# A fused attention, RWKV and feed-forward layer on one core: a new opening, new engine orders, and four second feed-forwards whose residual is added in SBUF

## The chip, the cores and the metric

The kernel runs on 1 core of one Trainium2 chip. The metric is the device time of one execution in microseconds (us). Before the change it is 283.79 us, the median of 3 runs (283.71 to 286.62).

## What is computed

Eight batches of 512 tokens with 128 channels pass through four blocks, each added to its own input. All data is f32.

```python
x = L0_attn_a_hidden_states                       # [8, 512, 128]
x = x + attn(_layernorm(x), W_q)                  # (y Wq^T) y^T y, without softmax
x = x + ffn(_layernorm(x), ...)                   # first feed-forward
x = x + rwkv(_layernorm(x), ...)                  # time mix with a scan over tokens, then channel mix
x = x + ffn(_layernorm(x), ...)                   # second feed-forward, same weights
...
def ffn(tgt):                                     # only expert 0 of 8 has weight 1
    h = relu(tgt @ w1 + b1)
    z = tgt + (h @ w2 + b2)
    return (z - mean(z)) * rsqrt(var(z) + 1e-5) * gamma + beta
```

## The kernel before, in words

One program runs on five in-order engines: TensorE (PE), VectorE (DVE), ScalarE (ACT), GpSimd (POOL) and the DMA queue of SyncE (SP). They meet by semaphores only. Nothing is scheduled by a compiler: each engine's part of the file ends in a long list of calls, written out by hand, such as `attn_gram(1, 3)`, which is batch 1 into PSUM bank 3. That list is the order in which the engine works. Extra arguments on PE's calls, such as `x1.ready(0)`, are waits for the former user of the bank.

The residual stream of batch b stays in SBUF in `R[b]`, 128 partitions by 4 groups by 128 channels. One batch goes through these stages:

- Attention: `attn_stats` and `mean_var` on DVE (L394, L422), `shift`, `power`, `bias` on POOL (L269, L293, L297; the reciprocal root and the bias of the norm), `attn_normed` on ACT, which writes XN (L678). Then PE: `attn_gram` (L918), `attn_transpose` (L906), `attn_proj` (L926) and `attn_apply` (L933), with copies out of PSUM on ACT between them, and `attn_out` on DVE (L428), which makes x1.
- A feed-forward (f1, later f2): the same norm gives y (`ffn_normed`), PE transposes it (`ffn_transpose`, L906), ACT evacuates it as yT and adds the centred bias B2C (L730). Four `hidden_up` (L945) and `relu` (L738) make h. The sum z = y + b2 + h W2 is collected in one bank: `ffn_start` (L952) transposes yT back into the bank, four small transposes, and four `ffn_down` (L961) of four products each add to it. DVE takes `z_stats` (L394), `mean_var`, and after POOL's `z_shift` (L288) and `power` (L293) `ffn_scaled` (L440), which writes zg. POOL issues a DMA that adds beta to R (`ffn_residual`, L321) and one that adds zg to R (`ffn_sum`, L329); for batch 0 of f1 and batch 7 of f2 DVE does the latter (`ffn_add`, L447). SP stores batch b when this is done.
- Time mix and channel mix: transposes and products on PE (L975 to L1020), scans and elementwise work on DVE, exponentials and squares on ACT, small norms and the adding DMAs (L337, L344) on POOL.

The opening: SP loads x0 of batches 0, 1 and 2 among the first weights. PE runs 42 transposes of the identity (`warm_up`, L1026), `centre_bias` (L1032) and then batch 0. `centre_down_bias` (DVE, L582) reads what `centre_bias` wrote. `ffn_y` has two copies per feed-forward, h has one.

Of the kernel before, what the change touches and what calls it, by code (L numbers as in the profile page):

```python
# [24 lines left out]
def hybrid_layer(nc, hidden, w_q, w1, w2, b1, wk, wv, wr, wo, f_wk, f_wr, f_wv, vectors, gamma, beta, out):  # L25
# [5 lines left out]
    with ExitStack() as ctx:  # L31
# [83 lines left out]


        class Norm:


            def __init__(self, n, dst=None, dst_name="", steps=("ve", "rs", "nb")):  # L120
# [6 lines left out]
                self.scale = Steps(n + "_scale_steps", 1, *steps)  # L127
                self.dst = dst
                if dst is not None:
                    self.nm = copies(n + "_nm", [P, J], 2)  # L130
                    self.nb = copies(n + "_nb", [P, J], 2)
                    self.ready = Steps(dst_name + "_ready", 1, "but last", "all")

        class Ffn:


            def __init__(self, n, stage, x):
                self.stage = stage
# [71 lines left out]
        def _(sp):  # L210
# [37 lines left out]
        def _(pool):  # L248
# [73 lines left out]

            def ffn_sum(b, f, tile):
# [7 lines left out]
            def cmix_sum(b):
# [19 lines left out]
            power(2, f1.norm); ffn_residual(1, f1); bias(2, f1.norm); shift(3, f1.norm); power(3, f1.norm)
            bias(3, f1.norm); ffn_residual(2, f1); ffn_residual(3, f1); z_shift(0, f1); power(0, f1.znorm)
            shift_twice(0); power(0, nt); back_shift(0); bias(0, nt); back_power(0); z_shift(1, f1); back_scale(0)
            power(1, f1.znorm); shift(4, f1.norm); power(4, f1.norm); ffn_sum(1, f1, f1.zg); bias(4, f1.norm)
            ffn_residual(4, f1); shift_twice(1); power(1, nt); back_shift(1); bias(1, nt); z_shift(2, f1)
            back_power(1); power(2, f1.znorm); back_scale(1); ffn_sum(2, f1, f1.zg); shift_twice(2); power(2, nt)
            tmix_residual(0); back_shift(2); back_power(2); shift(0, ncm); power(0, ncm); z_shift(3, f1); bias(0, ncm)
            back_scale(2); power(3, f1.znorm); shift(5, f1.norm); power(5, f1.norm); ffn_sum(3, f1, f1.zg)
            bias(5, f1.norm); bias(2, nt); ffn_residual(5, f1); z_shift(4, f1); power(4, f1.znorm); shift_twice(3)
            ffn_sum(4, f1, f1.zg); power(3, nt); bias(3, nt); back_shift(3); tmix_residual(1); back_power(3)  # L360
            shift(1, ncm); power(1, ncm); back_scale(3); bias(1, ncm); shift(6, f1.norm); power(6, f1.norm)
            shift_twice(4); bias(6, f1.norm); power(4, nt); shift(7, f1.norm); bias(4, nt); power(7, f1.norm)
            ffn_residual(6, f1); z_shift(5, f1); bias(7, f1.norm); power(5, f1.znorm); cmix_sum(0)
            ffn_sum(5, f1, f1.zg); shift(0, f2.norm); power(0, f2.norm); ffn_residual(7, f1); bias(0, f2.norm)
            shift_twice(5); z_shift(6, f1); ffn_residual(0, f2); power(6, f1.znorm); power(5, nt); bias(5, nt)
# [5 lines left out]
            shift_twice(7); power(7, nt); shift(2, f2.norm); bias(7, nt); power(2, f2.norm); tmix_residual(4)
            bias(2, f2.norm); back_shift(6); shift(4, ncm); power(4, ncm); ffn_residual(2, f2); bias(4, ncm)
            back_power(6); back_scale(6); z_shift(1, f2); power(1, f2.znorm); cmix_sum(3); ffn_sum(1, f2, f2.zg)
            shift(3, f2.norm); power(3, f2.norm); bias(3, f2.norm); back_shift(7); back_power(7); z_shift(2, f2)
# [805 lines left out]
```

## Time and profile before

| what | us |
|---|---|
| median of 3 runs | 283.79 |
| the profiled execution, its own time | 286.06 |
| its span, first to last instruction | 284.3 |
| PE busy | 263.8 (93%) |
| ACT busy | 229.8 (81%) |
| DVE busy | 227.1 (80%) |
| POOL busy | 148.5 (52%) |

The span is what the trace covers. The profiled execution's own time is 1.8 us longer than its span and 2.3 us above the median. A change is worked out in the span's microseconds and taken off the median. Ends of matmuls are modelled in the profile, so the distance from one start to the next is used as a matmul's cost.

### The profile page before, as it was taken

The numbers are of one execution on the slowest core, as the hardware profiler recorded it, in microseconds if no ns is written. First come the engines' busy times: TensorE is split into PE (matmuls) and PEld (weight loads), VectorE is DVE, ScalarE is ACT, GpSimd is POOL, SyncE is SP. The second block draws the span as 40 slices with busy tenths as digits, with TensorE's granted clock in tenths as the row PEclk, the third lists the DMA queues.
The fourth block names the chain that finished last, engine by engine and source line by source line (L and its number), as shares of the span: only waits on it lengthen the run. The fifth ranks groups of instructions, "written<-read, shape, count | busy, mean of one in ns | idle before, by whom it ended". The sixth has DMA issues, their size and how long they took to land. (4 is left out here: it accounts for less than half of the span.)

```text
span 284.3 us, 5322 instructions
## 1 busy us (share of the span) xinstructions
PE 263.8 (93%) x1556; PEld 196.6 (69%) x1556; DVE 227.1 (80%) x739; ACT 229.8 (81%) x443; POOL 148.5 (52%) x294
## 2 busy tenths in 40 slices
PE   7598999997996999999999999999999989999990
PEld 7598688566684577477665676866757848777770
DVE  1648616889999999999999999999998499754224
ACT  2486994966598989997999998998999998788630
POOL 3474934654192599285882661953922524851331
PEclk9959999999999999999999999999999999999997
DMA  6910340220124122244404303225351405643132
GB/s 185 310 53 0 56 81 15 40 37 13 24 39 75 26 51 37 39 76 74 74 1 77 74 16 60 37 47 105 55 108 26 75 0 110 115 98 78 25 61 74
DMA packets 17740, 18.10 MB, mean 64 GB/s; under 512 B 1456, under 2 KB 11568, under 8 KB 17712
## 3 DMA queue, kind: packets, MB, share of 16 engines
q0 software_dynamic: 6480, 11.80, 24.3%
q1 hardware_dynamic: 11232, 5.97, 7.4%
q8 instruction: 12, 0.20, 0.3%
q14 instruction: 16, 0.13, 0.1%
HBM read 3.87 MB, written 2.10 MB: 21 GB/s over the span
## 5 line engine op out<-in xcount | busy, mean ns | idle before, releaser
L961 PEld LDWEIGHTS bank<-W,f_h 128*128 128x128 f32 x512 | 61.3, 192 | 9.9 <-issue 9.2
L961 PE MATMUL bank<-W,f_h 128*128 128x128 f32 x512 | 63.1, 275 | 0.3 <-ACT f_h L738 0.3
L945 PE MATMUL bank<-f_yT,W 128*128 128x512 f32 x128 | 62.6, 599 | 0.1
L738 ACT ACTIVATE f_h<-bank,B1C 128x512 f32<-128x512 f32 x64 | 42.5, 684 | 9.5 <-PE bank L945 9.3
L1003 PE MATMUL bank<-XK,FWk 128*128 128x512 f32 x64 | 32.2, 607 | 2.8 <-DVE XK L559 1.4
L945 PEld LDWEIGHTS bank<-f_yT,W 128*128 128x128 f32 x128 | 21.7, 190 | 18.3 <-issue 12.3
L1009 PEld LDWEIGHTS bank<-FWv,KK 128*128 128x128 f32 x256 | 30.5, 192 | 4.8 <-issue 2.2
L1009 PE MATMUL bank<-FWv,KK 128*128 128x128 f32 x256 | 31.2, 276 | 0.2 <-ACT KK L799 0.2
L394 DVE BATCH_NORM_STATS2 f_zn_stats<-bank 128x6 f32<-128x128 f32 x64 | 14.1, 282 | 18.3 <-PE bank L961 18.2
L678 ACT ACTIVATE f_y<-R,f_yn_nb,f_yn_rs 128x128 f32<-128x128 f32 x64 | 26.3, 485 | 2.6 <-POOL f_yn_nb L297 2.3
L440 DVE SCALAR_TENSOR_TENSOR f_zg<-bank,f_zn_rs,GAMMA 128x128 f32<-128x128 f32 x64 | 17.9, 341 | 7.6 <-issue 5.6
L329 POOL DMA_DIRECT2D R<-f_zg x14 | 12.9, 920 | 19.1 <-DVE f_zg L440 19.1
L321 POOL DMA_DIRECT2D R<-BETA x16 | 14.4, 899 | 14.0 <-ACT f_y L678 13.6
L795 ACT ACTIVATE KK<-bank 128x512 f32<-128x512 f32 x32 | 18.8, 595 | 3.5 <-PE bank L1003 3.4
L799 ACT ACTIVATE KK<-KK 128x512 f32<-128x512 f32 x32 | 19.8, 634 | 0.3
L678 ACT ACTIVATE XN<-R,attn_nb,attn_rs 128x128 f32<-128x128 f32 x32 | 13.1, 485 | 8.6 <-POOL attn_nb L297 8.6
L293 POOL TENSOR_TENSOR f_zn_rs<-f_zn_ve,K_RSQRT 128x4 f32<-128x4 f32 x16 | 17.8, 1114 | 0.8
L1003 PEld LDWEIGHTS bank<-XK,FWk 128*128 128x128 f32 x64 | 10.4, 190 | 10.7 <-issue 5.1
L293 POOL TENSOR_TENSOR f_yn_rs<-f_yn_ve,K_RSQRT 128x4 f32<-128x4 f32 x16 | 16.7, 1046 | 0.0
L269 POOL TENSOR_TENSOR f_yn_ve<-f_yn_mv,K_EPS 128x4 f32<-128x4 f32 x16 | 4.1, 256 | 21.6 <-DVE f_yn_mv L422 21.6
L288 POOL TENSOR_TENSOR f_zn_ve<-f_zn_mv,K_EPS 128x4 f32<-128x4 f32 x16 | 5.7, 356 | 18.1 <-DVE f_zn_mv L422 17.9
L678 ACT ACTIVATE NC<-N,cmix_nb,cmix_rs 128x128 f32<-128x128 f32 x32 | 13.2, 488 | 2.1 <-POOL cmix_nb L297 2.1
(133 smaller groups left out, 619.2 us busy)
## 6 DMA issues: line engine op xcount, KB each, us to landing
R<-BETA POOLq DMA_DIRECT2D x16, 256.0 KB, 3.5
R<-f_zg POOLq DMA_DIRECT2D x14, 256.0 KB, 3.4
R<-in_hidden SPq DMA_DIRECT2D x8, 256.0 KB, 4.7
R<-N POOLq DMA_DIRECT2D x8, 256.0 KB, 3.3
out_x<-R SPq DMA_DIRECT2D x8, 256.0 KB, 2.3
R<-G POOLq DMA_DIRECT2D x7, 256.0 KB, 3.4
W<-in_w SPq DMA_DIRECT2D x2, 256.0 KB, 4.5
BETA<-in_beta SPq DMA_DIRECT2D x1, 256.0 KB, 5.2
```

The lines of the kernel that those rows point to most:

```text
L293: pool.tensor_tensor(n.rs[b % 2][:], n.ve[b % 2][:], K_RSQRT[:], ALU.pow).then_inc(n.scale.sem(b), 1)
L321: pool.dma_start(R[b][:], BETA[:], accum_op=ALU.add).then_inc(*f.xb.step(b))
L394: last = v.bn_stats(n.stats[b % 2][:, j, :], src[:, j, :])
L440: last = v.scalar_tensor_tensor(zg[:, j, :], z[:, j, :], f.znorm.rs[b % 2][:, j:j + 1], GAMMA[:], ALU.mult, ALU.mult)
L678: done = a.activation(dst[:, j, :], src[:, j, :], ACT.Identity, scale=n.rs[b % 2][:, j:j + 1], bias=n.nb[b % 2][:, j:j + 1])
L738: a.activation(at(f.h, b)[:, n, :], banks[bank][:], ACT.Relu, bias=B1C[:, n:n + 1]).then_inc(f.h_ready[n], 1)
L795: a.activation(at(KK, b)[:, n, :], banks[bank][:], ACT.Relu).then_inc(square[n].sem(b), 1)
L799: a.activation(at(KK, b)[:, n, :], at(KK, b)[:, n, :], ACT.Square).then_inc(square[n].sem(b), 1)
L945: t_.matmul(banks[bank][:], W1[:, n * P:(n + 1) * P], at(f.yT, b)[:], start=True, stop=True).then_inc(f.h_psum[n], 1)
L961: last = t_.matmul(banks[bank][:, j * C:(j + 1) * C], at(f.h, b)[:, n, j * P:(j + 1) * P], W2[:, n, :], start=False, stop=(n == H - 1), sk ...
L1003: t_.matmul(banks[bank][:], FWk[:, n * P:(n + 1) * P], at(XK2, b)[:], start=True, stop=True).then_inc(kk_psum[n], 1)
L1009: last = t_.matmul(banks[bank][:, j * C:(j + 1) * C], at(KK, b)[:, n, j * P:(j + 1) * P], FWv[:, n, :], start=(n == 0 and j == 0), stop=(n ...
```

## The change

- Opening. PE's 42 warm-up transposes become 24, then `centre_bias`, then 20. On DVE the statistics of batch 1 move ahead of `centre_down_bias`. XN of batch 0 is written by DVE (a new `attn_normed`) instead of ACT. SP loads x0 of batch 3 ahead of B1 and W1. Four batches, not seven, have their attention products ahead of the first `hidden_up`; batches 4 to 7 follow between feed-forwards.
- All engine orders, and the banks that PE uses, are written anew. y has four copies and h two. Some semaphores are split in two so that neighbouring batches can pass.
- In f2, for batches 1, 3, 5 and 6, `ffn_start` is gone. `ffn_down` opens the bank itself. A new POOL DMA `down_residual` adds b2 (as rows, B2R) onto y in SBUF once y is transposed. DVE adds the bank to y (`z_sum`), takes the statistics from SBUF and scales in place (`z_sum_scaled`).
- For f1 batch 0 and f2 batch 7, `ffn_scaled` and `ffn_add` become `ffn_gain`, one product with gamma that doesn't wait for the norm, and `ffn_out`, which scales and adds into R.
- B2R is made once: `bias_diagonal` on DVE, `down_bias_part` on PE, `down_bias_rows` on ACT.

```diff
-COPIES = {"N": 3, "f1_y": 2, "f2_y": 2, "f1_yT": 2, "f2_yT": 2, "XN": 3, "XNT": 2, "GRAM": 2, "PROJ": 2, "f1_zg": 3, "f2_zg": 3, "others": 1}
+COPIES = {"N": 3, "f1_y": 4, "f2_y": 4, "f1_yT": 2, "f2_yT": 2, "f1_h": 2, "f2_h": 2, "XN": 3, "XNT": 2, "GRAM": 2,
+          "PROJ": 2, "f1_zg": 3, "f2_zg": 3, "others": 1}
+SPLIT = {"f1": (0,), "f2": (7,)}
+IN_SBUF = {"f2": (1, 3, 5, 6)}
...
+            load_x0(3)
             sp.dma_start(B1[:], b1).then_inc(w1_loaded, DMA)
             sp.dma_start(W1[:], w1).then_inc(w1_loaded, DMA)
-            load_x0(3)
...
+            def down_residual(b, f):
+
+                if b == f.in_sbuf[0]:
+                    pool.wait_ge(b2_rows, 1)
+                pool.wait_ge(f.yT_psum, b + 1)
+                for earlier in f.yb.before(b):
+                    pool.wait_ge(*earlier)
+                pool.dma_start(at(f.y, b)[:], B2R[:], accum_op=ALU.add).then_inc(*f.yb.step(b))
...
+            def z_sum(b, f, bank):
+
+                dve.wait_ge(f.z_psum, b + 1)
+                dve.wait_ge(*f.yb.ready(b))
+                v.tensor_tensor(at(f.y, b)[:], bank_rows(bank), at(f.y, b)[:], ALU.add).then_inc(f.z_ready, 1)
...
+            def ffn_gain(b, f, bank):
...
+                v.tensor_tensor(at(f.zg, b)[:], bank_rows(bank), GAMMA[:].unsqueeze(1).broadcast_to([P, J, C]), ALU.mult).then_inc(f.zg_ready, 1)
+
+            def ffn_out(b, f):
+
+                dve.wait_ge(*f.znorm.scale.done(b, "rs"))
+                dve.wait_ge(f.zg_ready, b + 1)
+                dve.wait_ge(*f.xb.ready(b))
+                for j in range(J):
+                    last = v.scalar_tensor_tensor(R[b][:, j, :], at(f.zg, b)[:, j, :], f.znorm.rs[b % 2][:, j:j + 1], R[b][:, j, :],
+                                                  ALU.mult, ALU.add)
...
+            def attn_normed(b):
+
+                dve.wait_ge(na.mv_ready, b + 1)
+                dve.wait_ge(*na.scale.done(b, "rs"))
+                dst = at(XN, b)
+                for j in range(J):
+                    done = v.tensor_scalar(dst[:, j, :], R[b][:, j, :], na.mv[b % 2][:, j, 0:1], na.rs[b % 2][:, j:j + 1], ALU.subtract, ALU.mult)
...
+                    if b - len(f.y) in f.in_sbuf:
+                        act.wait_ge(*f.out.ready(b - len(f.y)))
...
-                    last = t_.matmul(banks[bank][:, j * C:(j + 1) * C], at(f.h, b)[:, n, j * P:(j + 1) * P], W2[:, n, :], start=False,
+                    last = t_.matmul(banks[bank][:, j * C:(j + 1) * C], at(f.h, b)[:, n, j * P:(j + 1) * P], W2[:, n, :], start=(n == 0 and j == 0 and b in f.in_sbuf),
```

PE from its start, before. IDENT x42 is the warm-up, XN alone is `attn_gram`, IDENT,XN is `attn_transpose`, GRAM,Wq is `attn_proj`, B2C,W is `bias_part`, PROJ,XNT is `attn_apply`.

```order
L1026 MATMUL bank<-IDENT 128x128 x42
L1032 MATMUL bank<-VEC,MEAN 128x1
L906 MATMUL bank<-IDENT,XN 128x128 x4
L918 MATMUL bank<-XN 128x128 x4
L906 MATMUL bank<-IDENT,XN 128x128 x4
L918 MATMUL bank<-XN 128x128 x4
L926 MATMUL bank<-GRAM,Wq 128x128
L1039 MATMUL bank<-B2C,W 128x1 x4
L906 MATMUL bank<-IDENT,XN 128x128 x4
L918 MATMUL bank<-XN 128x128 x4
L933 MATMUL bank<-PROJ,XNT 128x128 x4
```

The same place in the change, by the changed file's line numbers.

```order
L1113 MATMUL bank<-IDENT 128x128 x24
L1119 MATMUL bank<-VEC,MEAN 128x1
L1113 MATMUL bank<-IDENT 128x128 x20
L1005 MATMUL bank<-XN 128x128 x4
L993 MATMUL bank<-IDENT,XN 128x128 x4
L1013 MATMUL bank<-GRAM,Wq 128x128
L1132 MATMUL bank<-B2C,W 128x1 x4
L1020 MATMUL bank<-PROJ,XNT 128x128 x4
L993 MATMUL bank<-IDENT,XN 128x128 x4
L1005 MATMUL bank<-XN 128x128 x4
```

`centre_bias` moved into the middle of the warm-up, and batch 0 goes all the way to `attn_apply` ahead of anything of batch 1.

DVE from its start, before: statistics of a batch, their aggregation, `centre_down_bias` (B2C), then the next batches.

```order
L394 BN_STATS attn_stats<-R 128x6 x4
L422 BN_AGGR attn_mv<-attn_stats 128x2 x4
L582 TENSOR_TENSOR B2C<-VEC,bank 128x1
L394 BN_STATS attn_stats<-R 128x6 x4
L422 BN_AGGR attn_mv<-attn_stats 128x2 x4
```

DVE from its start in the change, down to `attn_out` of batch 0.

```order
L422 BN_STATS attn_stats<-R 128x6 x4
L460 BN_AGGR attn_mv<-attn_stats 128x2 x4
L422 BN_STATS attn_stats<-R 128x6 x4
L460 BN_AGGR attn_mv<-attn_stats 128x2 x4
L658 TENSOR_SCALAR XN<-R,attn_mv,attn_rs 128x128 x4
L644 TENSOR_TENSOR B2C<-VEC,bank 128x1
L422 BN_STATS attn_stats<-R 128x6 x4
L460 BN_AGGR attn_mv<-attn_stats 128x2 x4
L422 BN_STATS attn_stats<-R 128x6 x4
L460 BN_AGGR attn_mv<-attn_stats 128x2 x4
L466 TENSOR_TENSOR R<-bank,R 128x512
```

The one-column subtraction of B2C moved behind batch 1's statistics, and XN of batch 0 came to DVE. `attn_out` of batch 0 stands behind four batches' statistics instead of eight.

DVE at its end, before: z of batch 7.

```order
L394 BN_STATS f_zn_stats<-bank 128x6 x4
L422 BN_AGGR f_zn_mv<-f_zn_stats 128x2 x4
L440 SCALAR_TENSOR_TENSOR f_zg<-bank,f_zn_rs,GAMMA 128x128 x4
L447 TENSOR_TENSOR R<-f_zg,R 128x512
```

DVE at its end in the change, from `z_sum` of batch 6.

```order
L449 TENSOR_TENSOR f_y<-bank,f_y 128x512
L422 BN_STATS f_zn_stats<-f_y 128x6 x4
L460 BN_AGGR f_zn_mv<-f_zn_stats 128x2 x4
L508 SCALAR_TENSOR_TENSOR f_y<-f_y,f_zn_rs,GAMMA 128x128 x8
L422 BN_STATS f_zn_stats<-bank 128x6 x4
L460 BN_AGGR f_zn_mv<-f_zn_stats 128x2 x4
L475 TENSOR_TENSOR f_zg<-bank,GAMMA 128x512
L483 SCALAR_TENSOR_TENSOR R<-f_zg,f_zn_rs,R 128x128 x4
```

The wide operation now stands ahead of the four narrow ones, which need the norm's scale.

## Rows read from the trace of the kernel before

**Rows 1.** Windows: length, busy by engine, PE's granted clock (1.00 = 2.4 GHz), DMA share, GB/s.
```profile
9.00:13.54 4.54, 1.53 (x15) 1.34 (x14) 4.26 (x29) 1.31 (x4) 2.78 (x8) 1.00 1.12 314
13.54:20.50 6.96, 6.96 (x35) 6.88 (x36) 3.86 (x26) 6.78 (x20) 4.71 (x14) 0.53 0.29 86
20.50:32.26 11.76, 10.82 (x94) 10.44 (x93) 8.64 (x46) 8.24 (x23) 6.90 (x18) 0.99 0.06 10
32.26:60.00 27.74, 27.62 (x161) 19.57 (x160) 16.74 (x63) 21.15 (x46) 14.51 (x30) 1.00 0.31 54
60.00:92.00 32.00, 27.33 (x168) 20.43 (x168) 30.46 (x87) 25.04 (x47) 16.41 (x34) 1.00 0.19 33
92.00:250.00 158.00, 155.15 (x883) 109.78 (x883) 148.57 (x434) 146.90 (x270) 90.72 (x157) 1.00 0.32 58
```

In these rows the busy times are those of PE, PE's weight loads, DVE, ACT and POOL, in this order.

**Rows 2.** Timeline of PE: start, length, instruction [idle before <-releaser].
```profile
1.53 7.49 PE L1026 MATMUL bank<-IDENT 128*128 128x128 f32 x42 [1.53 <-POOL IDENT L251]
...
9.00 0.64 PE L906 MATMUL bank<-IDENT,XN 128*128 128x128 f32 x4
...
13.54 0.86 PE L906 MATMUL bank<-IDENT,XN 128*128 128x128 f32 x4 [3.01 <-ACT XN L678]
...
30.04 1.06 PE L933 MATMUL bank<-PROJ,XNT 128*128 128x128 f32 x8
30.93 0.60 PE L906 MATMUL bank<-IDENT,XN 128*128 128x128 f32 x4
...
32.26 3.96 PE L945 MATMUL bank<-f_yT,W 128*128 128x512 f32 x8
```

**Rows 3.** Timeline of DVE, opening.
```profile
9.18 0.16 DVE L582 TENSOR_TENSOR B2C<-VEC,bank 128x1 f32<-128x1 f32 x1 [4.11 <-PE bank L1032]
9.25 0.86 DVE L394 BATCH_NORM_STATS2 attn_stats<-R 128x6 f32<-128x128 f32 x4
...
24.52 0.88 DVE L596 TENSOR_SCALAR W<-W,W_MV 128x128 f32<-128x128 f32 x4
```

**Rows 4.** Timeline of ACT: XN of batch 1.
```profile
12.23 1.65 ACT L678 ACTIVATE XN<-R,attn_nb,attn_rs 128x128 f32<-128x128 f32 x4 [3.72 <-POOL attn_nb L297]
```

**Rows 5.** Timeline of POOL: the norm of batch 0, from its first step to its last.
```profile
5.22 0.20 POOL L269 TENSOR_TENSOR attn_ve<-attn_mv,K_EPS 128x4 f32<-128x4 f32 x1 [3.26 <-DVE attn_mv L422]
...
6.63 0.20 POOL L297 TENSOR_TENSOR attn_nb<-attn_nm,attn_rs 128x4 f32<-128x4 f32 x1
```

**Rows 6.** Timeline of PE at its end.
```profile
271.86 0.60 PE L952 MATMUL bank<-IDENT,f_yT 128*128 128x128 f32 x4
272.29 1.02 PE L945 MATMUL bank<-f_yT,W 128*128 128x512 f32 x2
273.15 3.73 PE L961 MATMUL bank<-W,f_h 128*128 128x128 f32 x32
```

**Rows 7.** Timeline of DVE at its end.
```profile
276.93 0.89 DVE L394 BATCH_NORM_STATS2 f_zn_stats<-bank 128x6 f32<-128x128 f32 x4 [3.68 <-PE bank L961]
...
279.71 1.12 DVE L440 SCALAR_TENSOR_TENSOR f_zg<-bank,f_zn_rs,GAMMA 128x128 f32<-128x128 f32 x4 [1.48 <-issue]
280.87 0.69 DVE L447 TENSOR_TENSOR R<-f_zg,R 128x512 f32<-128x512 f32 x1
```

**Rows 8.** DMA issues: KB each, median us from issue to landing.
```profile
R<-BETA POOLq DMA_DIRECT2D x16, 256.0 KB, 3.5
...
R<-in_hidden SPq DMA_DIRECT2D x8, 256.0 KB, 4.7
```

**Rows 9.** Waits: engine and line waited for, us in total, times, longest.
```profile
POOL tmix_tmp L278 <- DVE tmix_mv L422: 20.4, 6, 6.7
```

**Rows 10.** Groups by line and form: busy us, mean ns of one.
```profile
L269 POOL TENSOR_TENSOR cmix_ve<-cmix_mv,K_EPS 128x4 f32<-128x4 f32 x8 | 4.7, 593 | 1.0 <-DVE cmix_mv L422 1.0
...
L709 ACT ACTIVATE XNT<-bank 128x512 f32<-128x512 f32 x8 | 4.7, 586 | 0.0
...
L715 ACT ACTIVATE GRAM<-bank 128x128 f32<-128x128 f32 x8 | 2.0, 268 | 0.6 <-PE bank L918 0.4
```

More of the change, by code:

```diff
@@ L64, in ready, with before @@
                     return self.sem_added, self.added.index(b) + 1
-                return self.sems[b % 2], DMA * len([c for c in range(b % 2, b + 1, 2) if c not in self.added])
+                return self.sems[b % 2], DMA * len([c for c in self.moved if c <= b and c % 2 == b % 2])
+            def before(self, b):
+                same = [c for c in self.moved if c < b and c % 2 == b % 2]
+                return [self.ready(same[-1])] if same else []
         def copies(name, shape, count):
@@ L131, in __init__ @@
                     self.nb = copies(n + "_nb", [P, J], 2)
-                    self.ready = Steps(dst_name + "_ready", 1, "but last", "all")
+                    self.ready = Steps(dst_name + "_ready", len(dst) if n == "attn" else 1, "but last", "all")
         class Ffn:
-            def __init__(self, n, stage, x):
-                self.stage = stage
+            def __init__(self, n, x):
                 self.x = x
@@ L326, in ffn_sum @@
                 pool.wait_ge(*f.xb.ready(b))
-                if b >= 2:
-                    pool.wait_ge(*f.out.ready(b - 2))
+                for earlier in f.out.before(b):
+                    pool.wait_ge(*earlier)
                 pool.dma_start(R[b][:], at(tile, b)[:], accum_op=ALU.add).then_inc(*f.out.step(b))
@@ L334, in cmix_sum @@
                 pool.wait_ge(*x2u.ready(b))
-                if b >= 2:
-                    pool.wait_ge(*x3.ready(b - 2))
+                for earlier in x3.before(b):
+                    pool.wait_ge(*earlier)
                 pool.dma_start(R[b][:], at(G2, b)[:].rearrange("p (j c) -> p j c", j=J), accum_op=ALU.add).then_inc(*x3.step(b))
@@ L351, in _ @@
[L351 to L365, printed above, removed]
@@ L371, in _ @@
[L371 to L374, printed above, removed]
-            back_scale(7); power(2, f2.znorm); shift(5, ncm); tmix_residual(5); power(5, ncm); ffn_sum(2, f2, f2.zg)
@@ L386, in _ @@
+            ffn_sum(5, f2, f2.y); ffn_sum(6, f2, f2.y); z_shift(7, f2); power(7, f2.znorm)
         @block.vector
@@ L669, in _ @@
+            mean_var(7, f2.znorm); ffn_gain(7, f2, 6); ffn_out(7, f2)
         @block.scalar
@@ new lines, in _ @@
+            ffn_down(6, f1, 3, 6); tmix_transpose(4, 4); cmix_down(1, 3, 0); ffn_transpose(0, f2, 5)
+            hidden_up(7, f1, 2, 3, (m2_ready, 4)); hidden_up(7, f1, 3, 0, cgate.done(1, "kvs"))
+            hidden_up(0, f2, 0, 2, (f1.zg_ready, 6)); ffn_start(7, f1, 7, (f1.h_ready[0], 8)); hidden_up(7, f1, 1, 5)
+            cmix_transpose(2, 4); ffn_down(7, f1, 0, 7); hidden_up(0, f2, 2, 3, (f1.h_ready[2], 8))
+            product_k(4, 4, (xc_ready, 3)); hidden_up(0, f2, 1, 1, gate.done(3, "rl"))
@@ new lines, in _ @@
+            cmix_up(2, 0, 5, (f1.h_ready[1], 8)); cmix_up(2, 1, 2, (f2.h_ready[0], 1))
+            cmix_up(2, 3, 1, (f2.h_ready[1], 1)); product_o(3, 5, square[0].done(2, "relu"))
+            hidden_up(0, f2, 3, 4, expo.done(4, "diff")); ffn_start(0, f2, 2, square[1].done(2, "relu"))
+            cmix_down(2, 0, 3); ffn_down(0, f2, 0, 2); ffn_down(7, f1, 1, 7); product_v(4, 5)
+            gate_product(2, 1, square[3].done(2, "relu")); cmix_up(2, 2, 6, (f1.zg_ready, 7)); ffn_down(7, f1, 2, 7)
@@ new lines, in _ @@
+            cmix_down(3, 2, 0); ffn_transpose(2, f2, 7); cmix_down(3, 3, 0); cmix_up(4, 0, 1)
+            cmix_up(4, 1, 7, (f2.yT_ready, 3)); cmix_up(4, 3, 3, cgate.done(3, "rl"))
+            cmix_up(4, 2, 1, square[0].done(4, "relu")); hidden_up(2, f2, 1, 7, square[1].done(4, "relu"))
+            hidden_up(2, f2, 0, 3, square[3].done(4, "relu")); hidden_up(2, f2, 2, 0, cgate.done(3, "kvs"))
+            ffn_start(2, f2, 7, (f2.h_ready[1], 3)); product_o(5, 3, (f2.h_ready[0], 3)); cmix_down(4, 0, 1)
```

539 lines of the change are left out of this document (293 added, 246 removed).

## Prediction

> **What bounds the kernel now.** I read the stage windows first, because a share over the whole span mixes stages. Busy time beside length shows where PE is the limit [rows 1]: from 92 to 250 us PE is busy 155.2 of 158 us, from 32 to 60 us 27.6 of 27.7. DVE is close behind: 30.5 of 32 us from 60 to 92, 148.6 of 158 after that. So the kernel is PE's stream of products, with three kinds of loss. From 9.0 to 13.5 PE stands 3.0 us idle; from 13.5 to 20.5 it works at a granted clock of 0.53, a mix of 2.4 and mostly 1.2 GHz, which costs 6.96 x 0.47 = 3.3 us; from 20.5 to 32.3 another 0.9 is idle. From 60 to 92 it is idle 4.7 us, from 92 to 250 2.8. And the last product's result still passes DVE, POOL, DVE and the store.
>
> Next I read the timelines for the reason. PE's 3.01 us idle ends with XN of batch 1 [rows 2]. ACT started that XN at 12.23, let go by POOL's norm [rows 4], and that by DVE's statistics, which began only at 9.25: DVE had stood 4.11 us at the one-column B2C, whose PE product is queued behind 42 warm-up transposes [rows 3]. At the end PE's last four `ffn_down` end at about 276.9 [rows 6], and DVE's statistics, the scaled z and the addition into R follow [rows 7].
>
> **Prices, start to start.** Eight 128-column products: 30.04 to 30.93, 0.89 us [rows 2]. Four transposes: 271.86 to 272.29, 0.43. One `hidden_up`: 272.29 to 273.15, 0.86 [rows 6]. A projection 0.22 (a quarter of the eight), `bias_part` 0.8 at 2.4 GHz (taken from the size of the others; it stands on both sides of the sum and cancels). A norm on POOL: 5.22 to 6.83, 1.6 [rows 5]. XN on ACT 1.65 [rows 4], a 128x512 copy there 0.59, a 128x128 copy 0.27 [rows 10]; behind another instruction I count 0.1 less.
>
> **1. The opening, by hand.** Before, the first `hidden_up` starts at 32.26. Ahead of it from 9.00 lie 8 groups of transposes, 7 grams and 4 applies, 5 projections and `bias_part`: 3.4 + 9.8 + 1.1 + 0.8 = 15.1 us of work in 23.3 us, so 8.1 lost, against 7.2 that the windows account for.
>
> After, DVE doesn't stop at B2C. Statistics and aggregation are 0.86 + 0.38, so batch 1 is through about 1.2 us after its data. Its x0 is SP's second issue and takes 4.7 us in the median [rows 8], so some 6 us. XN(0) on DVE costs 0.88, by the nearest row of four 128x128 operations with a pointer scalar [rows 3]: ready at 8.1, and in time for 9.0 if x0 lands by 6.9. B2C comes behind it. The warm-up has 44 transposes for 42 at 7.49/42 = 0.18 us, so PE would be 0.4 late; but DVE is ready earlier than ACT was, and I leave the start at 9.0 (bounds 8.5 and 9.4). From there:
> - gram(0) to 9.9, transpose(0) 10.3, projection (GRAM copied meanwhile) 10.5, `bias_part` 11.3, apply(0) 12.2. XN(1) on ACT waits for PROJ(0)'s copy: 11.15 to 12.8, its norm long ready.
> - transpose(1) needs three quarters of it: 12.4 to 12.85, gram(1) 13.75. XN(2) to 14.4: transpose(2) 14.0, gram(2) 15.35, projection(1) 15.55. XN(3) 15.1 to 16.7: PE idle until 16.3, gram(3) 17.65, projection(2), apply(1) to 18.75.
> - y(0) follows XN(3) and two copies, 17.1 to 18.7: `ffn_transpose(0)` 19.2, apply(2) 19.4 to 20.3, projection(3), `hidden_up(0)` at **20.5**.
>
> This is 10.1 us of work (five transposes, 4 + 3 groups of eight, four projections, `bias_part`) in 11.5 us, 1.4 lost, the longest gap 0.75. Lead over before: 8.1 - 1.4 = **6.7 us**. This counts the clock as restored, since it fell after the 3 us gap and there is none so long. Work put off is still in the sum; it is not counted as won. Going on in the same way from 20.5 through PE's list to gram(5), about 23 us later, I find ACT never more than 1 us behind and PE with other products at that moment. Before, that kind of stretch (32 to 60) lost only 0.1. A relu held behind a y would cost up to its 1.65 once; kept for the range.
>
> **2. Four `ffn_start` gone.** 4 x 0.43 = **1.7 us** of PE, where PE is busy at 98%. For them DVE gets four `z_sum`, each about 0.69 like the 128x512 addition [rows 7], 2.8 us in all; the first two fall where DVE is at 94%, the last two at the end, where PE's work for batches 6 and 7 covers them. POOL gets four adding DMAs. A new wait: `z_sum` needs b2 landed in y, about 3.5 us after issue [rows 8]. Ahead of z lie four `hidden_up` and four `ffn_down`, 3.4 + 3.6 = 7.0 us. Cover 7.0 against 3.5: nothing. If it were gone, 3.5 each, 14 in all. A second: y(5) and y(7) reuse the copies of batches 1 and 3 and so wait for `ffn_sum` of those to land, 3.5 against the 1.6 + 0.9 of POOL's path between: up to 1.1 us each; PE has other work, I take nothing and keep 2.2 for the range. `ffn_start(7)` waits for `z_sum(6)`, 0.7, behind two `hidden_up`, 1.7: nothing.
>
> **3. The end.** `ffn_gain` runs in the 1.5 us in which DVE waited for POOL, `ffn_out` costs what `ffn_scaled` cost, 1.12, and the 0.69 of the addition is gone: **0.7 us** [rows 7]. In front of it the path from `cmix_down(7)` to y(7) takes about 6.4 us by the same durations, PE's cover is one `ffn_down`, four `hidden_up` and two `ffn_down`, 6.1: up to 0.3 lost, not counted.
>
> **4. The rest at nothing.** B2R once (0.2 PE, 0.3 DVE, 0.6 ACT), split semaphores, two copies of h (PE may run a batch ahead), banks. The reordering from 60 us on is unknown from the trace of before: at best it closes that window's 4.7 us, at worst opens as much again. I take zero.
>
> Sum: 6.7 + 1.7 + 0.7 = 9.1. The profiled execution would go from 286.1 to 277.0, its span from 284.3 to 275.2; taken off the median of the runs, 283.8 - 9.1 = **274.7 us**.
>
> **A rule against the change.** POOL's `cmix_ve` of 128x4 takes 593 ns in the mean [rows 10], the same form 200 ns in the opening when DVE is at rest [rows 5]: POOL is stretched beside a busy DVE. The added DVE work reads SBUF twice per instruction: 16 quarters of `z_sum_scaled` of some 0.28 us. If each stretched POOL by its length, that is 4.5 us of POOL time, and POOL is idle 67 of 158 us in the main stage; on the path at worst it makes 279.2, about the time of the second rival, whose chance holds it. The Trainium skill, SBUF — State Buffer, section Who interferes with whom, says that a DVE instruction with two SBUF inputs contends with a GpSimd one that reads SBUF; by that rule the trace agrees, and `ffn_gain`, with one SBUF input, would leave the last `power` alone.
>
> **Rivals.**
> - *The mid-stage gaps close too.* PE's losses of 60 to 92 us are waits for single results of ACT and DVE; time mix starts earlier against PE's stream and h no longer blocks. 274.7 - 4.7 = 270.0. Against it: DVE is at 95% there.
> - *DVE becomes the bound.* It is idle only 11 of 190 us from 60 to 250. If its stream decides, its added 2.8 + 0.9 + 0.3 = 4.0 us come off the lead: 278.7.
> - *The lead is given back.* XN and the copies of batches 5 to 7 (3 x 2.8 = 8.3 us of ACT) now fall into the busy stage, where ACT is idle 7.0 us of 32. If PE waits for all that was put off, the opening brings nothing: 283.8 - 2.4 = 281.4. Against it: ACT's idle 11 of 158 us later on.
> - *Slower: POOL's queue.* Each `down_residual` waits for a transpose on PE, and behind it stand `z_shift`, `power` and other batches' DMAs. POOL's waits for another engine reach 6.7 and are 3.4 us in the mean in the largest group [rows 9]. Four of 3.4, all reaching PE, are 13.6: 288.3. It decides from 3.0 us each, (9.1 + 2.8)/4. Against it: POOL's idle time, and y transposed early.
>
> **Chances.** As forecast 0.50 (its own range 272 to 277), gaps close 0.15, DVE bound 0.17, given back 0.10, slower 0.08. One per cent, about what a measurement of this kernel can tell, is 2.8 us. The first three are faster, with a sliver of the fourth: 0.83; same 0.10; slower 0.07. The range goes down to 269.5 and up to 281.0, which leaves out the slower case, half of the fourth and the edge of the second.
>
> **What would show it.** First gram at 8.5 to 9.4, first `hidden_up` near 20.5, granted clock 1.00 throughout after the warm-up, PE idle under 1.5 us between them: step 1. PE idle from 60 us on near 7.5 us: step 4; if under 4, the first rival; if DVE stands near 100% with PE waiting for it, the second. No idle of DVE before a `z_sum` put down to a DMA: step 2. DVE from the last aggregation to the last instruction 0.7 us shorter: step 3. The forecast is wrong if the lead at the first `hidden_up` is there and the end is not 9 us earlier, or if the clock falls again.

## The result, and the profile after

| | before | after |
|---|---|---|
| median in the same comparison, us | 283.8 | 266.2 (265.6 to 266.7) |
| ratio, 95% interval | | 0.936 [0.931, 0.942] |
| the profiled execution, us | 286.06 | 266.14 |
| its span, us | 284.3 | 264.3 |

The change takes 17.6 us off the median and 20.0 us off the profiled span. The forecast was 274.7 (269.5 to 281.0): right in sign, wrong by half of the gain. The changed kernel on later occasions gave 266.7 (265.5 to 267.1) and 265.8 (264.8 to 266.8).

The first line of the page after the change: busy time and share of the span (264.3 us) by engine.

```profile
PE 255.3 (97%) x1544; PEld 191.7 (73%) x1544; DVE 228.2 (86%) x748; ACT 227.2 (86%) x440; POOL 159.0 (60%) x298
```

PE is shown busy 8.5 us less, DVE 1.1 us more.

PE's timeline in the opening after the change, against [rows 2].

```profile
1.53 5.38 PE L1113 MATMUL bank<-IDENT 128*128 128x128 f32 x24 [1.53 <-POOL IDENT L264]
6.71 0.43 PE L1119 MATMUL bank<-VEC,MEAN 128*128 128x1 f32 x2
7.00 2.67 PE L1113 MATMUL bank<-IDENT 128*128 128x128 f32 x20
9.50 1.06 PE L1005 MATMUL bank<-XN 128*128 128x128 f32 x8
...
16.71 0.71 PE L993 MATMUL bank<-IDENT,XN 128*128 128x128 f32 x4 [0.35 <-ACT XN L758]
...
20.92 1.93 PE L1032 MATMUL bank<-f_yT,W 128*128 128x512 f32 x4
```

`attn_gram(0)` starts at 9.50, the first `hidden_up` at 20.92 instead of 32.26, and the only recorded gap between them is 0.35 us where 3.01 stood.

Waits of PE on other engines, each line with the us in all, the number of times and the longest. First before, then after.

```profile
PE bank L906 <- ACT XN L678: 3.0, 1, 3.0
PE bank L906 <- ACT f_h L738: 2.5, 2, 1.9
...
PE bank L1003 <- DVE XK L559: 1.4, 1, 1.4
PE bank L933 <- ACT PROJ L721: 1.3, 1, 1.3
PE bank L1003 <- DVE EA L498: 1.1, 2, 0.9
PE bank L918 <- DVE R L428: 0.9, 1, 0.9
...
```

```profile
PE bank L1113 <- POOL IDENT L264: 1.5, 1, 1.5
PE bank L993 <- ACT XN L758: 0.3, 1, 0.3
```

The second list is complete. None of the middle's waits, which stood in the kernel before, is left.

**Where the 20 us lie, by DVE's stream.** I cut both spans at two instructions that each kernel has: DVE's first statistics of the time mix (`tmix_stats(0)`) and its last channel-mix addition (`cmix_out(7)`). This gives a head, a middle and a tail. Windows, columns as in [rows 1]; before first.

```profile
0.00:46.30 46.30, 40.70 (x260) 35.84 (x261) 23.07 (x130) 31.73 (x79) 23.92 (x71) 0.93 0.43 108
46.30:262.40 216.10, 208.58 (x1211) 149.78 (x1210) 196.63 (x577) 190.44 (x352) 118.80 (x213) 1.00 0.30 55
262.40:284.30 21.90, 14.49 (x90) 10.94 (x88) 7.39 (x34) 7.59 (x13) 5.81 (x10) 0.91 0.26 59
```

```profile
0.00:35.20 35.20, 33.27 (x221) 28.60 (x222) 22.62 (x129) 22.95 (x56) 21.18 (x65) 1.00 0.48 127
35.20:242.20 207.00, 206.90 (x1239) 152.18 (x1237) 194.77 (x572) 197.12 (x372) 128.65 (x220) 1.00 0.32 57
242.20:264.30 22.10, 15.09 (x89) 10.90 (x87) 10.86 (x48) 7.17 (x13) 9.16 (x15) 0.91 0.66 135
```

Head 46.3 to 35.2, **11.1 us**. Middle 216.1 to 207.0, **9.1 us**: DVE idle 19.5 to 12.2, and 1.9 us less DVE work. Tail 21.9 to 22.1, although DVE has 3.5 us more to do there. In this cut the tail gains nothing, since it begins at a DVE instruction.

Within the middle, the part in which DVE is densest; before, then after.

```profile
60.00:210.00 150.00, 143.51 (x818) 101.40 (x817) 146.78 (x422) 136.08 (x252) 89.95 (x159) 1.00 0.29 52
210.00:262.40 52.40, 51.37 (x313) 38.52 (x313) 38.17 (x117) 45.68 (x85) 21.16 (x37) 1.00 0.36 67
```

```profile
60.00:220.00 160.00, 159.90 (x930) 115.20 (x929) 159.35 (x446) 154.99 (x288) 100.05 (x168) 1.00 0.32 57
220.00:242.20 22.20, 22.20 (x152) 18.02 (x152) 12.80 (x52) 19.36 (x39) 11.91 (x20) 1.00 0.43 80
```

After the change DVE is busy 99.6% for 160 us, where it was 97.9% for 150 us. Its idle time behind that stretch falls from 14.2 to 9.4 us.

### The profile page after: what moved, and what is told of

The parts are those of the page before. It is cut to its first block and busy times, and to the rows that moved or that the text cites. A ratio compares the mean times of both kernels' runs of the same rounds, so it can differ in the third digit from the quotient of the medians.

```text
span 264.3 us, 5318 instructions
## 1 busy us (share of the span) xinstructions
PE 255.3 (97%) x1544; PEld 191.7 (73%) x1544; DVE 228.2 (86%) x748; ACT 227.2 (86%) x440; POOL 159.0 (60%) x298
## 3 DMA queue, kind: packets, MB, share of 16 engines
HBM read 3.87 MB, written 2.10 MB: 23 GB/s over the span
## 5 line engine op out<-in xcount | busy, mean ns | idle before, releaser
L1048 PE MATMUL bank<-W,f_h 128*128 128x128 f32 x512 | 64.3, 275 | 0.0
L1096 PEld LDWEIGHTS bank<-FWv,KK 128*128 128x128 f32 x256 | 31.7, 192 | 5.0 <-issue 3.6
L1096 PE MATMUL bank<-FWv,KK 128*128 128x128 f32 x256 | 33.6, 275 | 0.0
L1090 PE MATMUL bank<-XK,FWk 128*128 128x512 f32 x64 | 30.7, 599 | 0.0
L882 ACT ACTIVATE KK<-KK 128x512 f32<-128x512 f32 x32 | 19.5, 625 | 0.1
L311 POOL TENSOR_TENSOR f_yn_rs<-f_yn_ve,K_RSQRT 128x4 f32<-128x4 f32 x16 | 18.6, 1161 | 0.0
L293 POOL TENSOR_TENSOR tmix_tmp<-tmix_mv,K_EPS 128x4 f32<-128x4 f32 x8 | 2.5, 310 | 25.4 <-DVE tmix_mv L460 25.4
L306 POOL TENSOR_TENSOR f_zn_ve<-f_zn_mv,K_EPS 128x4 f32<-128x4 f32 x16 | 7.5, 469 | 16.6 <-DVE f_zn_mv L460 16.6
L364 POOL DMA_DIRECT2D R<-G x7 | 7.4, 1050 | 14.7 <-DVE G L634 14.7
L422 DVE BATCH_NORM_STATS2 f_yn_stats<-R 128x6 f32<-128x128 f32 x64 | 13.8, 278 | 2.0 <-DMA R<-G 1.7
L758 ACT ACTIVATE N<-R,tmix_nb,tmix_rs 128x128 f32<-128x128 f32 x32 | 13.1, 482 | 0.9 <-POOL tmix_nb L315 0.9
```

Of the source, the lines that this page charges most:

```text
L311: pool.tensor_tensor(n.rs[b % 2][:], n.ve[b % 2][:], K_RSQRT[:], ALU.pow).then_inc(n.scale.sem(b), 1)
L422: last = v.bn_stats(n.stats[b % 2][:, j, :], src[:, j, :])
L758: done = a.activation(dst[:, j, :], src[:, j, :], ACT.Identity, scale=n.rs[b % 2][:, j:j + 1], bias=n.nb[b % 2][:, j:j + 1])
L882: a.activation(at(KK, b)[:, n, :], at(KK, b)[:, n, :], ACT.Square).then_inc(square[n].sem(b), 1)
L1048: last = t_.matmul(banks[bank][:, j * C:(j + 1) * C], at(f.h, b)[:, n, j * P:(j + 1) * P], W2[:, n, :], start=(n == 0 and j == 0 and b in ...
L1090: t_.matmul(banks[bank][:], FWk[:, n * P:(n + 1) * P], at(XK2, b)[:], start=True, stop=True).then_inc(kk_psum[n], 1)
```

## Experiments

"Middle" is the distance from `tmix_stats(0)` to `cmix_out(7)` in the profiled execution.

| run | median us | against its base | first tmix_stats | middle |
|---|---|---|---|---|
| before | 283.8 | | 46.3 | 216.1 |
| b_copies | 285.0 | ratio 1.000 | 46.4 | 216.1 |
| b_open | 281.5 | -2.2 | 41.7 | 217.6 |
| b_pe | 288.6 | +2.9 | 47.3 | 217.8 |
| b_lesspe | 284.9 | ratio 0.998 | 42.4 | 217.7 |
| b_dve | 293.2 | +7.5 | 44.2 | 222.5 |
| b_less | 283.1 | ratio 0.996 | 44.0 | 215.0 |
| after, again after2, after3 | 266.2, 266.7, 265.8 | | 35.2, 34.2, 34.9 | 207.0, 208.7, 207.0 |
| a_open | 269.9 | +3.2 | 38.8 | 207.0 |
| a_delay | 271.9 | +5.2 | 40.7 | 207.0 |
| a_pe | 269.4 | +3.2 | 34.6 | 210.2 |
| a_lesspe | 265.1 | -1.1 | 34.5 | 207.1 |
| a_dve | 272.2 | +6.0 | 33.8 | 214.2 |
| a_less | 264.5 | -1.7 | 34.7 | 206.0 |
| a_two | 267.6 | +1.8 | 34.4 | 209.1 |
| a_six | 266.9 | +1.1 | 35.1 | 208.9 |
| a_tail, again a_tail2 | 267.5, 266.6 | +1.8, +0.4 | 34.7, 34.4 | 208.6, 207.1 |

For b_ runs the base is the kernel before in the same comparison (283.7 to 286.0); the ratio stands where its interval holds 1 or nearly does. The median of b_copies counts an execution of 944.55 us; without it it is 284.2. For the a_ runs it is 266.2; for a_open and a_delay the 266.7, and for a_two, a_six and the first a_tail the 265.8, of the changed kernel beside them. Since that kernel itself moved between 265.8 and 266.7, and one a_ kernel by 0.9 between two occasions, I read no difference of medians under 1 us.

The middle of the changed kernel comes in two lengths. In after, after3, a_open, a_delay, a_lesspe and a_tail2 it is 207.0 to 207.1 us; in after2, the same kernel as after, it is 208.7. DVE's timeline of after2 shows the difference, a wait for the DMA that adds the channel mix's G to R, which the profile of after has nowhere near 180 us:

```profile
180.14 0.87 DVE L422 BATCH_NORM_STATS2 f_yn_stats<-R 128x6 f32<-128x128 f32 x4 [1.56 <-DMA R<-G]
```

a_tail (1.45 us) and a_two (1.57 us) have the same wait, a_pe, a_dve and a_less don't. So the middles of the latter are compared with 207.0, those of the former with 208.7.

### Which engine decides: work added

`hidden_up` with n = 1 gets four transposes of the identity in front (a_pe, b_pe), 16 times, 6.9 us.

```diff
+                if n == 1:
+                    for _ in range(4):
+                        t_.transpose(banks[bank][:, 0:P], IDENT[:], IDENT[:])
```

> The changed kernel with four more transposes of the identity on PE in front of one hidden_up of each batch and feed-forward: 16 groups of 0.43 us, 6.9 us of PE work, which nobody reads. Theory 1, PE is the bound from its first product to its last: +6.9 us (6.3 to 7.3). Rival, DVE is the bound in the middle: the groups fall partly into PE's waits for DVE, +2 to +5 us.

> The kernel before with the same 6.9 us of PE work. If before the change PE too was the bound nearly everywhere: +6 to +6.9 us. If PE then stood behind others' results from 60 us on, as 4.7 + 2.8 us of idle time say: +2 to +5 us.

DVE gets 12 additions of 128x512 into a spare tile (a_dve, b_dve): one per batch and a second for batches 2 to 5.

```diff
+                v.tensor_tensor(SPARE[:, b, :], WROW[:], WROW[:], ALU.add)
```

> The changed kernel with 12 more 128x512 additions on DVE, one in each batch's time mix and four more, 0.6 us each from start to start, 7.2 us of DVE work, which nobody reads. Theory 1, PE is the bound: 0 to +2 us. Rival, DVE is the bound in the middle: +5 to +7.2 us.

> The kernel before with the same 7.2 us of DVE work. If the lost time of 60 to 92 us and later came from a DVE that PE waited for: +4 to +7.2 us, far more than the changed kernel shows. If PE was the bound in both: 0 to +2 us as there.

A microsecond of PE costs 0.46 in the changed kernel (3.2 / 6.9) and 0.42 before. A microsecond of DVE costs 0.83 (6.0 / 7.2) and 1.04. The values of before are rough: by the ratios' intervals b_pe is 1.6 to 4.0 us slower (0.2 to 0.6 for each us) and b_dve 5.1 to 8.8 (0.7 to 1.2). Over the middle alone a_dve pays all of it (214.2 - 207.0 = 7.2) and a_pe 3.2. That speaks for DVE in both kernels, against the forecast's "PE's stream of products".

### Which engine decides: work taken away

> The changed kernel with the 128x1024 product that weights the scans' results done on a quarter of its width in all eight batches (the rest isn't computed): some 0.85 us less of DVE's work each, 6.8 us in all. Theory (DVE's stream decides most of the middle stretch, adding a DVE microsecond cost 0.83): -3.5 to -5.5 us, less than was added because PE at 97% is next. Rival (PE decides, DVE follows): 0 to -1.5 us.

> The kernel before with the same product on a quarter of its width in all eight batches (the rest isn't computed), 6.8 us less of DVE's work. Theory (in the old order the two engines wait for each other, adding a DVE microsecond cost 1.0): -4 to -6.5 us. Rival (PE decides): 0 to -2 us.

> The changed kernel with 14 of its 64 hidden_up products (one per batch, batches 0 and 1 of the first feed-forward excepted) on 256 of their 512 columns; the other half of that h isn't computed. 14 x 0.43 = 6.0 us of PE's work less. Taking 6.8 us of DVE's work away gave only 1.7. Theory (PE's stream is still the bound in the new order, as its 97% say): -4 to -6 us. Rival (both streams are full and tied to each other, so neither alone gives much): -1 to -2.5 us.

> The kernel before with the same 14 products on half their columns (the other half isn't computed), 6.0 us of PE's work less. Theory (PE's stream is the bound, with waits on top): -4 to -6 us. Rival (the old order's chain of waits decides): -1 to -2.5 us.

```diff
-                v.tensor_tensor(at(AB, b)[:, :, 0:T], ...
+                v.tensor_tensor(at(AB, b)[:, :, 0:P], ...
...
+                cols = T // 2 if n == 1 and (b >= 2 or f is f2) else T
+                t_.matmul(banks[bank][:, 0:cols], W1[:, n * P:(n + 1) * P], at(f.yT, b)[:, 0:cols], ...
```

The line of the weighting product in a_less: shortest, median and longest ns. In the changed kernel it took 1215.

```profile
L541 DVE TENSOR_TENSOR AB<-AB,EB x8: 382/412/427, 56.1 to 210.7; 128x256 f32<-128x256 f32 x8
```

That is 8 x 0.80 = 6.4 us less, for a middle 1.0 us shorter and a median 1.7 us lower; I had expected 3.5 to 5.5 us. So DVE leads by about 1 us in the new order, and something else stands right behind it. PE's amount of work alone doesn't decide either: with 6.0 us of products gone the middle stays at 207.1. In the old order the same two cuts give ratios of 0.996 [0.992, 1.000] and 0.998 [0.995, 1.002] where the theory expected 4 us or more. The windows of the middle, of a_lesspe and of a_less:

```profile
34.50:241.60 207.10, 205.80 (x1239) 151.51 (x1238) 194.86 (x572) 197.12 (x372) 128.57 (x220) 1.00 0.32 56
```

```profile
34.70:240.70 206.00, 205.80 (x1239) 152.03 (x1238) 189.60 (x573) 196.55 (x372) 127.01 (x220) 1.00 0.32 57
```

PE's busy time fell by 1.1 us when 6.0 us of products went, and its share stays at 99%. So time in which PE has nothing to do is partly shown as busy. A small case can be seen in PE's starts: before, the product at 63.41 is followed at 66.37, 2.96 us later for 0.86 us of work, 2.10 lost, of which 1.94 are recorded.

```profile
63.41 1.02 PE L945 MATMUL bank<-f_yT,W 128*128 128x512 f32 x2
66.37 0.66 PE L906 MATMUL bank<-IDENT,N 128*128 128x128 f32 x4 [1.94 <-ACT f_h L738]
```

The Trainium skill, Perfetto Trace Analysis, section Identifying the Most-Contended Engine, says that the busy share of matmuls is a poor measure of how near PE is to its limit, and to look at the weight loads' share. The runs agree that PE's busy share is a poor measure, since it stayed at 99% of the middle with 6.0 us less to do; the weight loads' share is 73% of the span beside PE's 97%. The same section takes the engine with the highest share as the one to work on first. For 160 us of the middle DVE was busy 99.6%, ACT 97%, and 6.4 us taken from DVE gave 1.7. The measurement decides: here the share named the leader, but not by how much it leads.

What stands behind DVE wasn't found. ACT is busy 197 of 207 us there, and no run changed its work; a chain through several engines would look the same. Nor was work taken from PE and DVE at once. Of DVE's 12.2 idle us in the middle the profile puts 6.3 down to waits for ACT, 2.8 to PE and 1.7 to the DMA that adds G to R.

### Copies or order

> The kernel before with two copies of h and four of y in both feed-forwards, orders untouched. The new order needs those copies; the question is whether they alone close gaps of the old order's middle stretch, from the time mix's first statistics to the last channel mix (216.1 us in the kernel before, 207.0 in the changed one). Theory (the order is what counts, and the copies only allow it): 0 to -1 us, middle stretch 215 to 217. Rival (the single copy of h made PE wait for the previous batch): -3 to -6 us, middle stretch 210 to 213.

```diff
-COPIES = {"N": 3, "f1_y": 2, "f2_y": 2, ...
+COPIES = {"N": 3, "f1_y": 4, "f2_y": 4, "f1_h": 2, "f2_h": 2, ...
```

Ratio 1.000 [0.996, 1.004], middle 216.1 as before. Copies alone do nothing for the old order. The new order can't be had with one copy of h, since its waits then go in a circle: PE's `hidden_up(3, f2, 1, 6)` waits for the relu of `hidden_up(3, f2, 2, 6)`, which would have to wait for `ffn_down(2, f2, 3, 7)`, and that stands behind it in PE's list. So the reverse wasn't tried. Over all runs without added work the old order's middle is 215.0 to 217.7 us, the new one's 206.0 to 209.1, whatever the opening and whatever was taken away.

No run keeps the new order and gives all eight `ffn_start` back, so their part of the middle's 9.1 us isn't measured by itself. Two signs say that it is small: 6.0 us of PE's products were worth 1.1, so 1.7 us of transposes would be worth some 0.3 (an estimate), and a_two, with two of the four given back, has a middle of 209.1 beside 208.7 for after2 with the same wait.

### The opening

> The changed kernel with one part of the opening undone: centre_bias behind all 44 warm-up transposes, and the B2C subtraction ahead of batch 1's statistics. B2C then runs near 9.5, batch 1's statistics to 10.7, XN(0) to 11.7, and the first gram starts near 11.7 instead of 9.5. Theory, what the head gains is carried to the end one for one: +2.2 us, or +4 to +5.5 if PE's 2 us of rest makes the granted clock fall again. Rival, the lead comes from the order of the later work alone: 0 to +1 us.

> The kernel before with only this part of the opening: centre_bias after 24 warm-up transposes, B2C behind batch 1's statistics, nothing else moved. PE's idle 3.0 us and the slow clock (3.3 us) should be gone and the first hidden_up 4 to 6 us earlier. If a lead in the head is carried: -4 to -6 us. If the waits of the old order in the middle eat it: 0 to -2 us.

> The changed kernel with 58 transposes of the identity on PE right in front of the first hidden_up, 6.3 us which nobody reads: the lead that PE had there is taken away, the order of all the rest stays. If DVE and PE are full from there on and the lead is carried: +5.5 to +6.3 us. If the new order of the middle alone makes the gain and the head has slack: 0 to +3 us.

```diff
-            warm_up(0, 24); centre_bias(); warm_up(0, 20)
+            warm_up(0, 44); centre_bias()
```

That is a_open on PE; on DVE `centre_down_bias()` goes ahead of batch 1's statistics. b_open does the reverse to the kernel before (24, `centre_bias`, 18), and a_delay puts 58 transposes, 6.3 us, ahead of the first `hidden_up`. Windows of a_open, then of b_open, around the place where the clock fell in [rows 1]:

```profile
9.00:12.00 3.00, 1.32 (x10) 1.33 (x11) 2.93 (x20) 0.04 (x1) 1.83 (x5) 0.94 1.05 319
12.00:18.00 6.00, 6.00 (x30) 6.00 (x29) 2.26 (x12) 4.55 (x12) 2.91 (x8) 0.50 0.68 192
```

```profile
9.00:20.00 11.00, 9.79 (x87) 9.44 (x86) 8.31 (x51) 9.41 (x29) 6.89 (x17) 1.00 0.65 187
```

With B2C behind the whole warm-up PE stands still and then works at 0.50 (1.2 GHz) for 6 us, without it the granted clock is 1.00. In a_open time mix starts at 38.8, in the changed kernel at 35.2 and, beside this run, 34.2; the end comes 3.2 us later. That lies between the two forecasts of the expectation, and two of the four executions of a_open have a mean granted clock of 0.98, two of 0.994 and more. In b_open time mix starts 4.6 us earlier, the profiled span is 3.1 shorter, and the median 2.2 (ratio 0.992 [0.989, 0.996]). a_delay starts time mix 5.5 to 6.5 us later and loses 5.2.

How much of b_open's 4.6 us is the clock can be read from runs whose edit leaves the opening alone. From 13.54 to 20.50 us the first row is b_less, the second b_lesspe, beside 0.53 in [rows 1]:

```profile
13.54:20.50 6.96, 6.96 (x53) 6.96 (x52) 4.71 (x28) 6.58 (x20) 4.98 (x15) 0.81 0.32 96
13.54:20.50 6.96, 6.59 (x59) 6.33 (x58) 5.67 (x36) 6.96 (x22) 4.99 (x13) 1.00 0.31 91
```

Time mix starts at 46.3 with 0.53, at 44.0 with 0.81 and at 42.4 with 1.00. PE's gap before that stretch is 3.01, 3.02 and 2.55 us, in a_open 2.44: its length alone doesn't say whether the clock falls. From PE's first attention product to time mix it is 37.3 us in before (9.00 to 46.3), 34.3 in b_lesspe (8.14 to 42.4) and 32.5 in b_open (9.20 to 41.7). So of b_open's 4.8 us in this stretch 3.0 are the clock of the one profile that it is compared with, and 1.8 remain where the clock didn't fall.

a_open and a_delay leave the middle at 207.0; b_open's is 1.5 us longer than that of before. There, and in b_lesspe (217.7), the granted clock from 60 to 70 us is 0.83 where it was 1.00, which is 10 x 0.17 = 1.7 us. So what the opening gives is mostly kept, and the middle's 9.1 us have another cause.

### y + b2 in SBUF, and the end

> The changed kernel with the second feed-forward of batches 5 and 6 as before: ffn_start back on PE (2 x 0.43 us, in the last stage), z taken from the bank, no z_sum and no down_residual for them; batch 7's z moves to bank 1. In the last stage PE is the bound by the windows of the changed kernel (20.0 of 20 us), DVE is half idle. Theory, PE decides there: +0.6 to +0.9 us. Rival, the DVE work saved (2 x 0.6 us) or the two DMAs saved count for more: 0 or less.

> The changed kernel with the second feed-forward of batches 2 and 4 in SBUF too, six instead of four: 2 x 0.43 us less on PE, 2 x 0.6 us more on DVE, two more adding DMAs on POOL. By the two probes a microsecond of DVE work costs 0.8 us and one of PE 0.5: -0.4 + 1.0, +0.5 us, at most half of it if batch 4 counts to the last stage. If PE is the bound: -0.9 us. If a b2 DMA comes late for its z_sum: +2 us and more.

> The changed kernel with batch 7's end as before: ffn_scaled and ffn_add instead of ffn_gain and ffn_out. The 128x512 operation is behind the norm's scale again: +0.7 us (0.5 to 0.8). Rival, the store hides it: 0.

> The changed kernel with the old form of the last batch's end (scaled, then added), the same kernel that gave 267.54 us before, +1.8 us on the changed kernel beside it, of which only some 0.7 lay behind PE's last product. If the other 1.1 us come from how one execution happens to interleave, the repeat gives 266.4 to 267.0. If the edit itself makes them, it gives 267.3 to 267.8 again.

```diff
-IN_SBUF = {"f2": (1, 3, 5, 6)}
+IN_SBUF = {"f2": (1, 3)}
...
-            ffn_gain(7, f2, 6); ffn_out(7, f2)
+            ffn_scaled(7, f2, 6); ffn_add(7, f2, f2.zg)
```

The first is a_two (`ffn_start` is back for batches 5 and 6, z of batch 7 in bank 1); a_six has 1 to 6 in SBUF. They are 1.8 and 1.1 us slower than four, but the second edit, a_tail, shows how little that means: it came out 1.8 slower, with a middle of 208.6 that its edit can't reach and that has the wait at 180 us, and the same kernel again, a_tail2, 0.4 slower, with 207.1 and without the wait. In a_six one b2 transfer did come late: DVE waits 1.00 us for it at 201 us. In size the SBUF form of single batches isn't settled.

The end on DVE's timeline, first of the changed kernel, then of a_tail2:

```profile
257.32 0.89 DVE L422 BATCH_NORM_STATS2 f_zn_stats<-bank 128x6 f32<-128x128 f32 x4 [2.78 <-PE bank L1048]
...
258.54 0.66 DVE L475 TENSOR_TENSOR f_zg<-bank,GAMMA 128x512 f32<-128x512 f32 x1
260.05 1.14 DVE L483 SCALAR_TENSOR_TENSOR R<-f_zg,f_zn_rs,R 128x128 f32<-128x128 f32 x4 [0.85 <-POOL f_zn_rs L311]
```

```profile
256.55 0.89 DVE L384 BATCH_NORM_STATS2 f_zn_stats<-bank 128x6 f32<-128x128 f32 x4 [2.78 <-PE bank L909]
...
260.50 0.69 DVE L466 TENSOR_TENSOR R<-f_zg,R 128x512 f32<-128x512 f32 x1
```

From the statistics to DVE's last end: 3.87 us with the new form, 4.64 with the old. From there to the end of the span, the store, 3.1 us (264.3 - 261.2) against 2.7 (263.9 - 261.2, and 284.3 - 281.6 before). So 0.77 us off DVE's chain leave 0.4 at the end of these profiles. POOL's last `power` takes 1.03 us in both, also where `ffn_gain` runs beside its first 0.2 us.

## Why the prediction was wrong, by its own steps

**Step 1, the opening: right in itself, read on the wrong engine.** The first `hidden_up` came at 20.92 for 20.5 forecast, clock 1.00, 1.3 us lost between for 1.4. PE's start was 9.50, not 9.0: the two extra transposes and the cut warm-up, 0.4 us, that I had worked out and dropped. The lead in PE's loss is 8.1 - 1.3 - 0.5 = 6.3 for 6.7. But "work put off is still in the sum; it is not counted as won" was too strict. Work of three batches' attention, 5.0 us of PE, moved behind the first `hidden_up`. DVE, which leads the middle, began time mix 11.1 us earlier: PE's 6.3, and about as much as was put off. That work then lay beside DVE's stream. It wasn't free there: at a_pe's 0.46 for each us, 5.0 us would cost 2.3 (an estimate; no run moves the attention back).

**Step 2, `ffn_start`: the wait as forecast, the worth too high as far as is known.** No idle time of DVE is put down to the b2 transfer in the changed kernel. Its landing takes 5.7 us, not the 3.5 I had assumed, against the cover of 7.0. The 1.7 us of PE were priced as if PE were the bound; 6.0 us of PE's products taken away were worth 1.1. DVE is shown busy only 1.1 us more in all, not 4.0, and 3.5 us of its work moved behind `cmix_out(7)`, where the tail is as long as before.

```profile
f_y<-B2R POOLq DMA_DIRECT2D x4, 256.0 KB, 5.7
R<-BETA POOLq DMA_DIRECT2D x16, 256.0 KB, 3.4
```

**Step 3, the end: right sign, half the size.** DVE's last stretch is 0.77 shorter, for 0.7 forecast, but from the start of DVE's last statistics to the end of the span it went from 7.3 to 7.0 us, 0.3. The term left out the store, which ends 3.1 us behind DVE where it ended 2.7 behind it before.

**Step 4, "the rest at nothing": this failed.** It was the term that made the forecast miss. By PE's starts, PE loses 11.9 us less behind the first `hidden_up` (20.0 - 6.3 - 0.3, less 1.5 of work that is gone). I had taken recorded idle time as the whole of what the order could give, 4.7 us between 60 and 92, and the rest of PE's 98% as work. The runs show in its place that the old order's middle is 215.0 to 217.7 us whatever copies it has and whether DVE or PE has 6 us less to do. So neither engine's amount of work set it, but waits that come with the order. The new order's middle is 9.1 us shorter: 7.3 us less idle time of DVE and 1.9 us less of its work there. Which waits of the old order they were isn't shown.

**The rivals.** The sign for "the mid-stage gaps close too" came true: PE's recorded idle after 60 us went from 7.5 to 0.1 us up to PE's last product. Its mechanism is what happened, its size (4.7) was half of the middle's gain. The sign for "DVE becomes the bound" came true by half: DVE stands at 99.6%, but no wait of PE for DVE is recorded, and a_dve had to show that DVE leads. Its consequence was wrong: I charged it all of DVE's added work and forgot that a DVE-led kernel gains from an earlier start of DVE's stream. The slower rival and "given back" didn't show; POOL has 40% idle. POOL is busy 159.0 us instead of 148.5, 8.0 of them issuing the four b2 DMAs, but no wait of PE for POOL is recorded behind the opening. So the rule against the change cost nothing that these rows show.

**The median.** The gain in the span, 20.0 us, was not the median's, 17.6. The profiled execution of before had a mean granted clock of 0.981; executions of the same kernel at 0.988 took about 283.7 us and one at 0.995 took 282.1. The spans at 0.988 are 281.4 to 282.4 us, 281.8 in the median, and 281.8 - 264.3 = 17.5 is about the median's 17.6. So some 2.5 of the 20.0 us belong to the slow clock of the one profiled execution. The 3.3 us of slow clock in the sum were thus only partly in the median, and I should have taken them off it only in part.

## What to carry to other kernels

- Cut a pipelined kernel at instructions of the engine that might lead, and compare stretches between the same two instructions. A lead at one engine's milestone is not the lead at another's (here 6.3 us of PE's loss and 11.1 us of DVE's start), and work put off costs less than its length if it lands beside a stream that leads.
- A PE share of 97% said nothing here on how far PE is from its limit; add work to an engine and take some away. Where adding costs its full length and removing gives nearly nothing, as with DVE here, less work for that engine alone won't shorten the kernel.
- Price a rewritten order by a range, not by zero, and open upwards: here 7.5 us of recorded idle time stood beside 11.9 us that PE lost less.
- Profile the same kernel more than once. One wait of 1.6 us and a slow clock in the opening came and went between executions, and either is as large as what most of these runs were to measure.

## What I had not expected of the hardware

- The granted clock differs between executions of one program. In 13 executions of the kernel before its mean was 0.977 to 0.995, the times 286.3 to 282.1 us. After the change it was 0.991 to 0.995 in four executions of the same comparison, and the times spread over 1 to 2 us instead of 3 to 4. In the profiles of the old opening the stretch from 13.54 to 20.50 us stood at 0.53, 0.81 or 1.00; in the changed kernel, without PE's gap at 10.5 us, it stood at 1.00. Putting the gap back (a_open) brought the variation back, 0.978 to 0.997. A gap isn't always followed by a fall: after 1.94 us idle at 64 us the kernel before went on at 1.00, after 1.95 us idle at 60 us b_open had 0.83 over ten us.
- An adding DMA of 256 KB within SBUF took 5.7 us to land for y and 3.4 for R, in one kernel and on one queue. Three of the four y transfers stand right behind another DMA in POOL's list, the fourth two small operations behind one; whether that is the cause wasn't tried.
